# Decoder layer on one core: attention outputs divided by their softmax sums without transposes

## What is computed

```python
scores = jnp.einsum('bhqd,bhkd->bhqk', q, k) * scale
att = jax.nn.softmax(scores, axis=-1)
y = jnp.einsum('bhqk,bhkd->bhqd', att, v)      # 16 heads of 16 channels
y = y.transpose(0, 2, 1, 3).reshape(b, t, c)
return y @ Wc
```

## Time and profile before

| | |
|---|---|
| Median of 3 runs | 1296.25 us (1288.26 to 1298.76) |
| The profiled execution | 1295.45 us, its span 1293.7 us |
| PE busy | 1144.6 us, 88% of the span |
| DVE busy | 969.7 us, 75% |
| ACT busy | 713.2 us, 55% |
| POOL busy | 530.1 us, 41% |

### The profile page before, as it was taken

One profiled execution on the slowest core, in us unless ns is written; L12 is line 12 of the kernel. 1 busy time (PEld: TensorE's weight loads), 2 busy tenths in 40 slices (PEclk: granted clock), 3 DMA queues, 4 the chain that ended last, 5 costly groups with the idle time before them and its releaser, 6 DMA issues. The chain is left out here.

```text
span 1293.7 us, 21922 instructions
## 1 busy us (share of the span) xinstructions
PE 1144.6 (88%) x7616; PEld 683.2 (53%) x7616; DVE 969.7 (75%) x2633; ACT 713.2 (55%) x1429; POOL 530.1 (41%) x728
## 2 busy tenths in 40 slices
PE   5699999999999999999999999999996218999994
PEld 2454545555455554544445454545333217888984
DVE  6678788788888778888888887878861577666551
ACT  6035555545555556676767676666773104565561
POOL 4656375654758443434242424240212003454332
PEclk9669899899999999999999999999999558999997
DMA  5551533515335243342525252415110504454322
GB/s 169 114 116 33 117 85 80 115 35 131 84 99 126 91 115 98 102 100 81 116 66 116 66 115 67 99 54 112 34 42 25 185 4 164 111 112 119 98 26 25
DMA packets 89330, 117.94 MB, mean 91 GB/s; under 512 B 12065, under 2 KB 59105, under 8 KB 89090
## 3 DMA queue, kind: packets, MB, share of 16 engines
q1 hardware_dynamic: 83074, 107.97, 32.5%
q0 software_dynamic: 6144, 8.52, 4.0%
HBM read 48.63 MB, written 16.91 MB: 51 GB/s over the span
## 5 line engine op out<-in xcount | busy, mean ns | idle before, releaser
L785 ACT ACTIVATE probs<-ps_st 128x512 f32<-128x512 f32 (+3 forms) x1024 | 476.5, 518 | 269.6 <-PE ps_st L618 265.6
L638 PE MATMUL ps_p<-kst,qst 63*128 63x512 f32 (+3 forms) x1024 | 383.5, 436 | 9.7 <-DVE mx L895 8.0
L618 PE MATMUL ps_st<-qst,kst 64*128 64x512 f32 (+3 forms) x1024 | 360.1, 419 | 9.2 <-ACT probs L785 8.4
L893 DVE TENSOR_REDUCE mx<-ps_p 128x1 f32<-128x512 f32 x512 | 322.3, 681 | 43.0 <-PE ps_p L638 42.2
L618 PEld LDWEIGHTS ps_st<-qst,kst 64*128 64x128 f32 x1024 | 165.9, 187 | 261.7 <-ACT probs L785 199.9
L895 DVE CUSTOM_DVE_ANT_0 ps_p<-ps_p,tri 128x128 f32<-128x128 f32 (+3 forms) x512 | 238.1, 515 | 13.7 <-PE ps_p L638 12.6
L599 PE MATMUL ps_o<-probs,vals 128*32 128x512 f32 (+3 forms) x2048 | 234.4, 530 | 14.6 <-POOL probs L508 14.6
L638 PEld LDWEIGHTS ps_p<-kst,qst 63*128 63x128 f32 x1024 | 172.5, 189 | 35.3 <-DVE mx L895 15.8
L450 POOL TENSOR_SCALAR lnw<-mv 128x4 f32<-128x4 f32 x24 | 5.1, 211 | 337.1 <-DVE mv L879 337.0
L508 POOL TENSOR_SCALAR_AFFINE_SELECT probs<-probs 128x512 f32<-128x512 f32 x128 | 79.2, 635 | 85.9 <-ACT probs L785 85.5
L1278 PE MATMUL moe_ps_y<-moe_w,moe_hid_h 128*128 128x256 f32 x512 | 94.6, 283 | 0.0
(11 more groups left out here) (224 smaller groups left out, 1893.5 us busy)
## 6 DMA issues: line engine op xcount, KB each, us to landing
qst<-qk_h SPq DMA_DIRECT2D x64, 256.0 KB, 4.7
kst<-qk_h SPq DMA_DIRECT2D x64, 256.0 KB, 4.9
qst<-qk_l SPq DMA_DIRECT2D x32, 256.0 KB, 5.4
kst<-qk_l SPq DMA_DIRECT2D x32, 256.0 KB, 4.9
moe_w1r<-in_w_dram SPq DMA_DIRECT2D x8, 1024.0 KB, 5.0
moe_w2r<-in_w_dram SPq DMA_DIRECT2D x8, 1024.0 KB, 9.9
xin<-in_x_dram SPq DMA_DIRECT2D x8, 512.0 KB, 4.1
xres<-in_x_dram SPq DMA_DIRECT2D x8, 512.0 KB, 3.9
```

The costliest lines, as they stand in the source:

```text
L618: last = nc.tensor.matmul(out, kst[rows, t % 2, pair, kt * P:(kt + 1) * P], qst[rows, t % 2, pair, lo:S], start=True, stop=not masked)
L638: last = nc.tensor.matmul(ps_p1[:, i % 3, 0:keys], qst[rows, t % 2, pair, qt * P:(qt + 1) * P], kst[rows, t % 2, pair, 0:keys], start=True ...
L785: nc.scalar.activation(probs[:, kt, j, 0:n], ps_st[:, i % 2, 0:n], ACT.Exp, scale=float(DH) ** -0.5).then_inc(exp_done, 1)
L893: nc.vector.tensor_reduce(mx[:, g % 2, at:at + 1], bank, AX.X, ALU.max).then_inc(max_done, 1)
```

## The change

Groups are taken in pairs (an even one and the odd one behind it), and a pair's outputs are divided where they lie, heads on partitions.

- A pair of heads gets 48 columns in `vals`: 16 values of the even group's head, 16 ones, 16 values of the odd group's head. An even group's `pv` reads columns 0 to 31 (values, ones), an odd group's columns 16 to 47 (ones, values). So in an even group's `ps_o` the upper half of each 32 partitions holds 16 copies of the sum, in an odd group's the lower half.
- `half_of` has two columns, 1 on one half of each 32 partitions and 0 on the other. After an even group ACT copies `ps_o` twice, scaled by either column, to `num` (which is `oraw`) and `den` (in `ocomp`).
- After an odd group the new step `divide` runs on DVE at place 16 (g + 1) + 13: two `scalar_tensor_tensor` add the other halves to `num` and `den`, `stream_shuffle` moves each half onto the other, then `reciprocal` of 128x512 and a product. The next group's first `pv`, at +14, waits for the two additions (`o_odd`).
- `high` at +15: ACT copies `num` to `ot_h`. `low` at +17: DVE makes `ot_l`. `y` waits for it.
- `og` and `ot` are gone, on PE, ACT and DVE, and the tile `rec` with them. The orders of value columns and of the rows of `Wc` and `w_o` are changed on the host to suit.

```diff
-        put(16 * (g + 1) + 15, "og", g)
+        if g % 2:
+            put(16 * (g + 1) + 13, "divide", g // 2)
+            put(16 * (g + 1) + 15, "high", g // 2)
+            put(16 * (g + 1) + 17, "low", g // 2)
...
-        put(after + 3, "ot", t, 0)
-        put(after + 19, "ot", t, 1)
...
                             if kt == 0 and g > 0:
-                                pe.wait_ge(o_raw, g)
+                                if g % 2:
+                                    pe.wait_ge(o_even, (g + 1) // 2)
+                                else:
+                                    pe.wait_ge(o_odd, g // 2)
...
-                        at = VW * (GH * (g % GROUPS) + j)
+                        at = VB * (GH * (g % GROUPS // 2) + j) + DH * (g % 2)
...
-                    elif kind == "og":
-                        pe.wait_ge(o_raw, s[1] + 1)
-                        for qt in range(TT):
-                            last = nc.tensor.transpose(bank[:, qt * P:(qt + 1) * P], oraw[:, qt * P:(qt + 1) * P], ident[:, :])
-                    elif kind == "ot":
...
-                elif kind == "pv" and s[2:] == (TT - 1, GH - 1):
+                elif kind == "pv" and s[1] % 2 == 0 and s[2:] == (TT - 1, GH - 1):
+
                     g = s[1]
                     act.wait_ge(pv_done, g + 1)
...
+                    nc.scalar.activation(num, ps_o[:, :], ACT.Copy, scale=half_of[:, 0:1])
+                    nc.scalar.activation(den, ps_o[:, :], ACT.Copy, scale=half_of[:, 1:2]).then_inc(o_even, 1)
+                elif kind == "high":
+                    n = s[1]
+                    act.wait_ge(o_divided, n + 1)
...
+                    nc.scalar.activation(ot_h[:, n % KT, :], num, ACT.Copy).then_inc(o_high, 1)
...
+                    elif kind == "divide":
+                        n = s[1]
+                        dve.wait_ge(pv_done, 2 * n + 2)
+                        dve.wait_ge(o_even, n + 1)
+                        nc.vector.scalar_tensor_tensor(out=num, in0=ps_o[:, :], scalar=half_of[:, 1:2], in1=num, op0=ALU.mult, op1=ALU.add)
+                        nc.vector.scalar_tensor_tensor(out=den, in0=ps_o[:, :], scalar=half_of[:, 0:1], in1=den, op0=ALU.mult,
+                                                       op1=ALU.add).then_inc(o_odd, 1)
+                        dve.wait_ge(o_odd, n + 1)
+                        link(nc.vector.stream_shuffle(moved, den, [i ^ 16 for i in range(32)]))
+                        link(nc.vector.reciprocal(moved, moved))
+                        nc.vector.tensor_tensor(out=num, in0=num, in1=moved, op=ALU.mult).then_inc(o_divided, 1)
+                    elif kind == "low":
+                        n = s[1]
+                        dve.wait_ge(o_high, n + 1)
+                        nc.vector.tensor_tensor(out=ot_l[:, n % KT, :], in0=num, in1=ot_h[:, n % KT, :].bitcast(F32),
+                                                op=ALU.subtract).then_inc(o_low, 1)
```

More of the change, by code:

```diff
@@ L30 @@
 ST_ROWS = 64
-VW = DH + 1
-VROW = H * VW + 16
+VB = 3 * DH
+VROW = PAIRS * VB
 BIG = float(2 ** 30)
@@ L59, in high_first @@
 def high_first(s):
-    return s[0] in ("xt", "ot") or (s[0] == "qk" and is_cross(s[1]) and s[2] == 1) or by_scalar(s)
+    return s[0] == "xt" or (s[0] == "qk" and is_cross(s[1]) and s[2] == 1) or by_scalar(s)
 def by_scalar(s):
@@ L276, in attention @@
         pv_done = sem("pv_done")
-        o_raw = sem("o_raw")
+        half_made = sem("half_made")
+        o_even = sem("o_even")
+        o_odd = sem("o_odd")
+        o_divided = sem("o_divided")
+        o_high = sem("o_high")
+        o_low = sem("o_low")
         res_bias = sem("res_bias")
@@ L694, in run @@
                         last = nc.tensor.transpose(bank[0:16, 0:P], mx[:, g % 2, :], ident[:, :])
-                    elif kind == "og":
-                        pe.wait_ge(o_raw, s[1] + 1)
-                        for qt in range(TT):
-                            last = nc.tensor.transpose(bank[:, qt * P:(qt + 1) * P], oraw[:, qt * P:(qt + 1) * P], ident[:, :])
-                    elif kind == "ot":
-                        t, k = s[1:]
-                        evicted(pe, ("og", GROUPS * t + 1 + 2 * k))
-                        for qt in range(TT):
-                            last = nc.tensor.transpose(bank[:, qt * P:(qt + 1) * P], ocomp[:, qt, k * P:(k + 1) * P], ident[:, :])
                     elif kind == "y":
                         t = s[1]
-                        evicted(pe, ("ot", t, 1))
+                        pe.wait_ge(o_low, KT * (t + 1))
                         if t == 0:
@@ L797, in step @@
                         nc.scalar.activation(xt_h[:, s[2], :], bank, ACT.Copy).then_inc(h_done, 1)
-                    elif kind == "ot":
-                        nc.scalar.activation(ot_h[:, s[2], :], bank, ACT.Copy).then_inc(h_done, 1)
                     elif kind == "xt3":
@@ L811, in step @@
                         for i in range(2):
-                            out = vals[:, t % 2, 2 * s[2] + i, 0:H * VW].rearrange("p (h e) -> p h e", e=VW)[:, :, 0:DH]
-                            last = nc.scalar.activation(out, bank[:, i * C:(i + 1) * C].rearrange("p (h d) -> p h d", h=H), ACT.Copy)
+                            out = vals[:, t % 2, 2 * s[2] + i, :].rearrange("p (m u d) -> p m u d", u=3, d=DH)[:, :, 0:3:2, :]
+                            last = nc.scalar.activation(out, bank[:, i * C:(i + 1) * C].rearrange("p (m u d) -> p m u d", u=2, d=DH), ACT.Copy)
                         last.then_inc(h_done, 1)
@@ L903, in run @@
                         dve.wait_ge(h_done, HI[s] + 1)
-                    if kind in ("xt", "ot"):
-                        hi, lo = (xt_h, xt_l) if kind == "xt" else (ot_h, ot_l)
-                        nc.vector.tensor_tensor(out=lo[:, s[2], :], in0=bank, in1=hi[:, s[2], :].bitcast(F32),
+                    if kind == "xt":
+                        nc.vector.tensor_tensor(out=xt_l[:, s[2], :], in0=bank, in1=xt_h[:, s[2], :].bitcast(F32),
                                                 op=ALU.subtract).then_inc(m_free, 1)
@@ L943, in run @@
                         for i in range(2):
-                            out = vals[:, t % 2, 2 * s[2] + i, 0:H * VW].rearrange("p (h e) -> p h e", e=VW)[:, :, 0:DH]
-                            src = bank[:, i * C:(i + 1) * C].rearrange("p (h d) -> p h d", h=H)
+                            out = vals[:, t % 2, 2 * s[2] + i, :].rearrange("p (m u d) -> p m u d", u=3, d=DH)[:, :, 0:3:2, :]
+                            src = bank[:, i * C:(i + 1) * C].rearrange("p (m u d) -> p m u d", u=2, d=DH)
                             last = nc.vector.tensor_copy(out, src)
```

41 lines of the change are left out of this document (21 added, 20 removed).

## The result

Measured together, the kernel before has a median of 1293.88 us (1288.26 to 1298.76, 4 runs) and the changed one 1492.08 (1478.07 to 1493.39, 4 runs). The ratio is 1.151, 95% interval 1.142 to 1.160. The forecast was 1460, 32 us too low and inside its range. That it came so close is partly luck: the waits were put too high by about as much as PE's clock was put too low.

The account below looks back on a forecast made before the run. PE was taken to set the pace in both attentions. Waits less spared transposes gave 62 us in cross-attention and 80 in self-attention, the clock 25: 167 us on 1295.45, said as 1460, range 1380 to 1540.

Parts of the forecast that it names:

- The reciprocal: On DVE, once a pair: 512 columns take 3.44 us, bounds 0.69 and 5.6 us.
- rival 3: On DVE: the wide reciprocal is a plain pass of 0.69 us, the second wait shrinks, 1366 us; chance 0.09.
- Rival 2: On DVE: the reciprocal takes eight steps a column, 4.4 us, lengthening the second wait, 1494 us; chance 0.13.
- Additions, shuffle, product: DVE's other new work per pair: two additions of 0.75 us, a shuffle of 0.74, a product of 0.69.
- The surcharge beside a busy POOL: On DVE's product of two SBUF tiles: 0.3 us more in self-attention, nothing in cross-attention.
- PE spared: 45 us: On PE: transposes of og and ot go, 1.4 us a pair, 45 us over 32 pairs.
- The two new waits: PE stands at pv +14 for 3.0 (cross) or 3.4 us (self), at p1 +17 for 2.3 or 3.0, per pair.
- The clock: PE's granted clock falls after the waits in both attentions, costing 0.8 us a pair, 25 us.
- rival 1: PE's clock falls unhidden at every pair, 3.2 instead of 0.8 us a pair, 1537 us; chance 0.12.
- PE busy near 45 us less: Sign expected in the changed kernel's profile: PE's busy time falls by about 45 us.
- DVE has 146 idle us, it can't all be hidden.: On DVE: 165 us of added work exceed its 146 us of idle time, so some must show.
- ACT's copies at no cost: On ACT: three whole-width copies of 0.60 us a pair either way, cost 0; 0.6 us a pair if cover fails.

Follow-up runs that it names:

- f1_apart: Kernel before plus one spare DVE reciprocal a pair of groups, in four pieces of 128 columns at +13, +17, +21, +25: 1338.69 us.
- f2_near: Kernel before plus one spare DVE reciprocal a pair of groups, in four pieces of 128 columns at +13, +14, +15, +16: 1395.33 us.
- e6_extra: Kernel before plus one spare, uncut DVE reciprocal of 128x512 a pair of groups at +13, which no instruction waits for: 1399.95 us.
- e10_bare: e2_act with DVE's two additions, shuffle, reciprocal and product replaced by a bare signal, outputs not divided: 1284.85 us.
- e7_spread: e2_act with DVE's instructions for the division set one at a time between maxima, the reciprocal in four pieces of 128 columns: 1457.18 us.
- e5_warm: Changed kernel plus useless fp32 products on PE in its waits, three before each even group's first pv, two before the waiting p1: 1472.94 us.
- e2_act: Changed kernel, but ACT copies the odd group's ps_o to SBUF, pv waits for that copy and DVE adds from SBUF: 1541.56 us.
- f3_spread_warm: e7_spread plus one useless PE product at each of the two places where e5_warm has its fills: 1482.74 us.

## Why the prediction was right, and where it was off

The direction, the places of the two waits and most prices held. Two terms of the sum were far off, the waits and the clock, and their errors cancel.

To find them, put the two stages of attention together, in us. PE runs the same instructions in the first four rows, and the same ones in the last five apart from the fills.

| | length | PE busy | PE not busy | DVE busy | DVE idle | clock in self, cross |
|---|---|---|---|---|---|---|
| before | 906 | 871 | 35 | 752 | 154 | 0.95, 1.00 |
| f1_apart | 945 | 900 | 45 | 851 | 94 | 0.93, 0.99 |
| f2_near | 1006 | 931 | 75 | 857 | 149 | 0.90, 0.95 |
| e6_extra | 1012 | 919 | 93 | 847 | 165 | 0.92, 0.94 |
| e10_bare | 887 | 830 | 57 | 723 | 164 | 0.93, 1.00 |
| e7_spread | 1058 | 951 | 107 | 925 | 133 | 0.80, 0.94 |
| e5_warm | 1070 | 993, 157 of it fills | 77 | 905 | 165 | 0.93, 0.98 |
| the change | 1092 | 933 | 159 | 911 | 181 | 0.80, 0.90 |
| e2_act | 1137 | 937 | 200 | 921 | 216 | 0.79, 0.88 |

- **The whole sum.** Against before, PE waits 124 us more in the changed kernel. Its transposes are gone, which is 41 us of its busy time (e10_bare). The instructions that are left take 933 - 830 = 103 us longer than in e10_bare, with the granted clock down. The rest of the span is 12 us longer. That makes 124 - 41 + 103 + 12 = 198, the measured difference. The clock accounts for the 103: reckoned as under e5_warm, the change spends 322 us at 1.2 GHz and e10_bare 59, and 263 us at half speed, with PE busy 85% of the time, are an estimated 110 us of work. The prediction had 187 of waits, 45 spared, 25 for the clock and nothing for the rest: 63 too much and 78 too little, so 1460 is near 1492 by luck.
- **The reciprocal.** Taken as 3.44 us by the slope of two small ones, measured 3.353, 107 us for 32. The bounds of 0.69 and 5.6 both fell, and with them rival 3 (plain pass). Rival 2's 4.4 us, the rule of eight steps a column from "VectorE: DVE Perf Modes" (section on the fixed hardware budget) in the Trainium skill, fell too: its time of 1494 nearly met the result, but its mechanism isn't there. A time that fits doesn't prove a cause.
- **Additions, shuffle, product.** 0.744, 0.74 and 0.75 us against 0.75, 0.74 and 0.69 (0.99 in self-attention). The total on DVE is +171 us against +165. The surcharge beside a busy POOL was put in the wrong stage. In self-attention every product but one took 0.69, though POOL is busy half of the time; the other slow ones, 0.83 to 1.11, are in cross-attention, and so are five of the six `ot_l` of 1.9 to 2.5 us, for which nothing was added. Each slow one has a wide instruction of POOL beside it at that very moment; POOL's busy share says little about that.
- **PE spared: 45 us.** As PE's busy time the term is right, 41 measured. As time off the end it isn't: e10_bare gains 7 us, since more than half came back as waits, mostly for ACT's exponentials. That PE was 97% busy didn't mean that its partners had room for a faster PE.
- **The two new waits.** The first, 3.0 and 3.4 us, 102 in all, measured 2.8 on average over 30, 84 in all. The second, 2.3 and 3.0 us, 85 in all, measured 2.42 on the timeline above; but over the whole run PE waits only 33 us more for the maxima (42.2 - 9.0), about 1 us a pair. So the second wait is the mis-sized one. It was added to the first as if both had their own cause, and e2_act shows that they share one debt.
- **The clock.** 25 us were taken, by the reasoning that a fall which begins in the first wait lies mostly under the second. In PE's own time it was 103 us, which is what rival 1 took (3.2 us a pair, 102 in all), and its sign, PEclk near 0.8, did appear in self-attention. So rival 1 had this term right and missed by the waits. For the same reason the sign "PE busy near 45 us less" failed: PE is busy 69 us more. How much the end would get back from a clock that stays up is another question: e5_warm gave 19 us, and can't tell whether the fills ate the rest. The low clock in rows 10 also lasts a little longer than was read: 0.64 from 139 to 140 puts its end near 139.7, not 139.4. And the wait of 0.63 us isn't the only idle time of PE ahead of it: from 132 to 133 PE was busy for 0.81 us.
- **"DVE has 146 idle us, it can't all be hidden."** True, but none of it was hidden. f2_near and e6_extra keep DVE's idle time at 149 and 165 us; only f1_apart, with the work far apart, uses 60 us of it.
- **ACT's copies at no cost.** Both scaled copies take 0.69 us instead of 0.60. The longer waits of `st` for ACT don't point to them: of 60 in the two stages, 2 follow a scaled copy within 4 us.

What is shown: DVE's five instructions make the whole loss (e10_bare), a load on DVE that nothing waits for makes 108 us of it (e6_extra), and its spacing decides how much (f1_apart, f2_near). That 160 us of added work go with 186 us of stage length is no law: e2_act and e7_spread have the same work on DVE within 4 us and lie 84 us apart.

What stays open: how the loss divides between PE's waits and its low clock as causes. Counted from before or from e10_bare, slower products are 43 to 74% of what the stages grew in every row but e5_warm, also in e7_spread, where the waits are short. The fills that raise the clock also take PE's time, so neither e5_warm nor f3_spread_warm settles it.

No complete kernel here beats the kernel before, and it is unlikely that an order of these instructions would. DVE's own work in the two stages is 421 + 490 = 911 us in the changed kernel, and the two stages of the kernel before are 906 us long. At these durations even a DVE that never idles would only draw level, and the run that idles least in these stages has 94 us.

## What to carry to other kernels

Before moving work onto a partner of the bottleneck engine, compare that partner's *new total* with the *old length* of the stage; here 911 against 906 us leave nothing to gain. A total that fits proves little, though: e6_extra has 847 us on DVE and still lost 108. Idle time of the partner can be used only if the work comes in pieces that it can catch up on between, within the lead that the buffers give: the same 121 us cost 47 us four places apart and 104 us in a row. And a wait that is taken away comes back at the next buffer as long as the debt is there (e2_act). When a sum of waits meets the measured time, compare the busy time of the same instructions too: here 103 us of slower products hid behind it.

## What the runs showed of the hardware

- The reciprocal on DVE: 250 ns for 16 columns, 353 for 32, 943 for 128 and 3353 for 512. From 32 to 512 that is 6.25 ns a column; four pieces of 128 cost 0.42 us more than one of 512.
- The same subtraction `ot_l` of two SBUF tiles took 675 to 2512 ns in the changed kernel (median 684), and the product 691 to 1114. All twelve over 0.72 us ran beside an instruction of POOL on 128x256 or more, and 51 of the other 52 with nothing of POOL beside them: at 846.86 `ot_l` took 2.51 us beside a POOL product of 128x1024 that ran 2.37 us from 846.45. `ot_l` reading PSUM took 692 before. The "GPSIMD Engine Reference" of the Trainium skill (specifications) has the SBUF interfaces shared with DVE for instructions with two SBUF inputs; these overlaps agree.
- With the same instructions PE was busy 830 us at a granted clock of 0.93 and 1.00 (e10_bare) and 951 us at 0.80 and 0.94 (e7_spread), though no wait for a maximum there was over 1.3 us.
- Switching between logarithm and exponential cost ACT 1283 ns each way, 64 times.
